# P·V of a cross-attention in four 32-column strips of the array instead of two of 64

## What is computed

```python
def _L0_xattn_ref(query, key, value, mask, Wq, bq, Wk, bk, Wv, bv, Wo, bo):
    Q = query @ Wq.T + bq
    K = key @ Wk.T + bk
    V = value @ Wv.T + bv
    Q, K, V = (z.reshape(b, -1, H, DK).transpose(0, 2, 1, 3) for z in (Q, K, V))   # H = 16, DK = 32
    scores = jnp.einsum('bhqd,bhkd->bhqk', Q, K) / jnp.sqrt(jnp.float32(DK))
    scores = jnp.where(mask == 0, -jnp.inf, scores)
    weights = jax.nn.softmax(scores, axis=-1)
    attn = jnp.einsum('bhqk,bhkd->bhqd', weights, V)          # "P·V"
    return attn.transpose(0, 2, 1, 3).reshape(b, -1, D) @ Wo.T + bo
```

## Time and profile before

| | before |
|---|---|
| median of 3 runs | 831.83 us (830.19 to 832.76) |
| the profiled execution | 832.76 us |
| its span | 831.0 us |
| TensorE busy | 787.1 us (95%), 8448 matmuls |
| VectorE busy | 624.2 us (75%) |
| ScalarE busy | 475.0 us (57%) |
| GpSimd busy | 274.7 us (33%) |

### The profile page before, as it was taken

How to read it: one execution, slowest core, us unless ns; L and a number is a source line. 1 busy time by engine, 2 the same in 40 slices (tenths; PEclk the granted TensorE clock), 3 DMA queues, 4 the chain that set the end, 5 groups by cost and what they waited for, 6 DMA issues and landing times.

```text
span 831.0 us, 21636 instructions
## 1 busy us (share of the span) xinstructions
PE 787.1 (95%) x8448; PEld 521.5 (63%) x8448; DVE 624.2 (75%) x971; ACT 475.0 (57%) x864; POOL 274.7 (33%) x411
## 2 busy tenths in 40 slices
PE   4999999999999999999999999994999999999994
PEld 2544455554445555545558544563999999999993
DVE  6866888889887767777765667988789688778850
ACT  3626666565765555566545034257578876876840
POOL 1422444433344333234421000031122474275342
PEclk9999999999999999999999999995999999999998
DMA  9444233444323344432323411113999898798201
GB/s 337 153 164 106 47 85 78 104 104 105 85 55 94 80 104 104 104 67 66 90 40 62 197 51 51 50 52 112 335 396 419 298 357 329 284 347 323 106 31 42
DMA packets 93148, 124.93 MB, mean 150 GB/s; under 512 B 75711, under 2 KB 78335, under 8 KB 81840
## 3 DMA queue, kind: packets, MB, share of 16 engines
q1 hardware_dynamic: 90528, 117.35, 44.1%
q0 software_dynamic: 2576, 7.02, 2.3%
HBM read 100.17 MB, written 6.88 MB: 129 GB/s over the span
## 4 chain that ended last, share of the span: by engine, by line
PE 74%; DVE 9%; ACT 5%; issue 4%; DMA 4%; POOL 2%; another core or an unknown queue 0%; POOLq 0%; ACTq 0%; DVEq 0%
PE bank L1333 56%; PE bank L1656 9%; PE bank L1445 3%; PE bank L1458 2%; DVE arena L837 2%; ACT arena L611 2%; DMA arena<-l_dram,arena 2%; DMA arena<-arena 2%; ACT arena L688 2%; DVE arena L976 2%; DVE arena L982 1%; PE bank L1346 1%; POOL arena L581 1%; POOL out L559 1%; ACT arena L797 1%
## 5 line engine op out<-in xcount | busy, mean ns | idle before, releaser
L1333 PE MATMUL bank<-arena 128*128 128x160 f16 (+8 forms) x4016 | 593.1, 308 | 7.8 <-DVE arena L1231 2.0
L1333 PEld LDWEIGHTS bank<-arena 128*128 128x128 f16 (+3 forms) x4016 | 339.2, 100 | 249.8 <-issue 13.2
L611 ACT ACTIVATE arena<-arena 128x2048 f16<-128x2048 f32 (+3 forms) x293 | 252.3, 905 | 11.7 <-DMA arena<-in_wq_t 6.7
L611 ACT ACTIVATE arena<-bank 128x512 f16<-128x512 f32 (+2 forms) x207 | 111.1, 543 | 206.5 <-PE bank L1333 131.8
L837 DVE SCALAR_TENSOR_TENSOR arena<-arena 128x2048 f16<-128x2048 f32 (+2 forms) x95 | 198.8, 2116 | 27.2 <-ACT arena L611 24.4
L837 DVE SCALAR_TENSOR_TENSOR arena<-bank,arena 128x512 f16<-128x512 f32 (+1 forms) x174 | 117.9, 685 | 70.6 <-ACT arena L611 66.9
L1656 PE MATMUL bank<-arena 128*128 128x160 f16 x1536 | 109.4, 233 | 1.0 <-issue 0.9
L1656 PEld LDWEIGHTS bank<-arena 128*128 128x128 f16 x1536 | 106.4, 98 | 1.8 <-issue 1.0
L559 POOL DMA_INDIRECT out<-arena x16 | 57.1, 3571 | 108.6 <-DVE arena L1263 106.2
L497 POOL TENSOR_TENSOR arena<-arena 32x1024 f16<-32x1024 f32 (+1 forms) x16 | 32.8, 2049 | 150.0 <-PE bank L1445 146.7
L688 ACT ACTIVATE arena<-arena 128x257 f32<-128x257 f32 x128 | 63.6, 498 | 25.6 <-DVE arena L984 25.6
(11 more groups left out here) (99 smaller groups left out, 418.1 us busy)
## 6 DMA issues: line engine op xcount, KB each, us to landing
arena<-in_w SPq DMA_DIRECT2D x64, 1024.0 KB, 5.7
arena<-in_ctx_t SPq DMA_DIRECT2D x16, 1024.0 KB, 5.2
arena<-in_awt SPq DMA_DIRECT2D x3, 1024.0 KB, 7.2
l_dram<-arena SPq DMA_DIRECT2D x4, 512.0 KB, 3.6
x_dram<-arena SPq DMA_DIRECT2D x1, 2048.0 KB, 12.4
arena<-in_x_t SPq DMA_DIRECT2D x2, 512.0 KB, 4.4
arena<-in_wq_t SPq DMA_DIRECT2D x1, 1024.0 KB, 6.6
arena<-in_x_t SPq DMA_DIRECT2D x1, 1024.0 KB, 8.7
```

Source lines behind the costliest of these rows:

```text
L611: return a.activation(dst, src, ACT.Copy, scale=scale)
L1333: last = m.matmul(out_ap, w, x, start=(n == 0), stop=(n == len(pairs) - 1))
```

## The change

P·V is cut into the 32-column strips of the array: each pair is four matmuls, each with 32 columns of w and the 32 columns of x of the same head, into the strip's 32 partitions of BG. `at` picks the head's place in x, since the scores lay their heads swapped in odd chunks. The bank then holds only wanted values, 256 columns. The evictions to `att_st` cover 128x256, and GpSimd moves each part with one copy of 128x256; two of its waits go, and `att_copied` counts one per step.

```diff
-        att_st = [xa.take([KC, PB, 2, S], F16) for _ in range(2)]
+        att_st = [xa.take([KC, PB, S], F16) for _ in range(2)]
...
-        pv_rows = BG[:].rearrange("p (c b h q) -> p c b h q", b=PB, c=KC, h=2)
+        pv_rows = BG[:, 0:PAIRS * S].rearrange("p (c b q) -> p c b q", b=PB, c=KC)
...
-            def attention_rows(m, last=False):
-
-                if last:
-                    pool.wait_ge(s["p_last_ready"], 2 * STEPS)
-                else:
-                    pool.wait_ge(s["vl_ready"], m + 2)
-                pool.sem_inc(s["pool_waits"], 1)
+            def attention_rows(m):
+
                 pool.wait_ge(s["pv_free"], m * 2 + 2)
                 pool.sem_inc(s["pool_waits"], 1)
                 for n in range(2):
-                    for r in range(HC):
-                        own = slice(r * DK, (r + 1) * DK)
-                        g.tensor_copy(attT[n][own, :, bass.ds(m * (PB * S), PB * S)]
-                                      .rearrange("p c (b q) -> p c b q", b=PB), att_st[n][own, :, :, r % 2, :]
-                                      ).then_inc(s["att_copied"], 1)
-                pool.wait_ge(s["att_copied"], m * (2 * HC) + 2 * HC)
-                pool.sem_inc(s["pool_waits"], 1)
+                    last = g.tensor_copy(attT[n][:, :, bass.ds(m * (PB * S), PB * S)],
+                                         att_st[n].rearrange("p c b q -> p c (b q)"))
+                last.then_inc(s["att_copied"], 1)
...
-                    act.wait_ge(s["att_copied"], from_zero(st * (2 * HC) - 2 * HC))
+                    act.wait_ge(s["att_copied"], from_zero(st - 1))
...
-                        cols = slice((c * PB + b) * HALF, (c * PB + b + 1) * HALF)
+                        cols = slice((c * PB + b) * S, (c * PB + b + 1) * S)
                         for n, (w, x) in enumerate(pairs):
-                            for r in range(2):
-                                own = slice(r * HALF, (r + 1) * HALF)
-                                at = (r + c) % 2
-                                last = m.matmul(BG[own, cols], w[:, own], x[:, at * HALF:(at + 1) * HALF],
+                            for r in range(HC):
+                                own = slice(r * DK, (r + 1) * DK)
+                                at = (r + 2 * (c % 2)) % HC
+                                last = m.matmul(BG[own, cols], w[:, own], x[:, at * S:(at + 1) * S],
                                                 start=(n == 0), stop=(n == len(pairs) - 1))
                     last.then_inc(s["pv_ps"], 1)
...
-            pe.wait_ge(s["att_copied"], STEPS * (2 * HC))
+            pe.wait_ge(s["att_copied"], STEPS)
```

More of the change, by code:

```diff
@@ L536, in _ @@
             step(STEPS - 1, nxt=False)
-            attention_rows(STEPS - 1, last=True)
+            attention_rows(STEPS - 1)
             def l2_lo(t):
```

## The result

| | before | after |
|---|---|---|
| median of 7 runs | 831.83 us (830.19 to 834.63) | 839.56 us (837.44 to 841.73) |
| ratio | | 1.0083, 95% interval 1.006 to 1.0104 |
| the profiled execution, its span | 832.76, 831.0 us | 838.28, 836.4 us |

The change makes the kernel 0.8% slower by the ratio, 7.7 us (0.9%) by the medians of seven and 5.4 us by the spans of the two profiled executions. Five further runs of the changed kernel on record lie between 836.55 and 841.33 us. The forecast was 828.9 us with a range from 826.5 to 836.

The account below looks back on a forecast made before the run. TensorE's work was taken to bound each step. Savings of 1.3 us (12 steps), 0.7 (steps 4, 6), 0.4 (step 15) and 0.5 (step 16), together 2.9, gave 828.9 us against the median of 831.83; range 826.5 to 836.

Parts of the forecast that it names:

- The bound: Whole step of the loop: it is as long as its TensorE work, 24.40 us; removing GpSimd's copies alone gives nothing.
- The strips overlap, 25 ns a group: P·V's matmuls: four strips run beside each other, a group takes 25 ns instead of 31.7, P·V 1.40 us.
- The supply of instructions: TensorE's queue in P·V: an instruction costs at most 5 ns, taken as 3; a group has eight instructions.
- My formula: P·V if supply binds: 448 instructions less 50 queued, times the time of each, plus 0.12; 2.1 us at 5 ns.
- What is late next: Scores after P·V wait for VectorE's fourth k_lo: start at 1.78 us, not 1.52, so 0.11 us saved a step, not 0.37.
- The chain of the evictions: Shorter evictions bring transposes for P·V's second half earlier; steps 4, 6 and 16 gain 0.6 us even without faster matmuls.
- 12 × 0.11: Steps 1 to 3, 5 and 7 to 14: each saves 0.11 us, together 1.3 us.
- supply becomes the bound: Rival, chance 0.18: TensorE's queue limits P·V from 4 ns an instruction; kernel 3 us slower at 5 ns, 10 at 6.
- My 3.7 us: Time the present P·V's 224 instructions would take by the skill page's 20-cycle floor, set against 1.89 us in the trace.

## Why the prediction was wrong, point by point

- **The bound was read rightly.** TensorE sets the step; removed copies and shorter evictions gave nothing in steps that had no stall.
- **The strips overlap, 25 ns a group: right.** Three strips run at 25.0 ns, and the first seven groups of the change do.
- **The supply of instructions: the step that failed in the steady state.** I bounded one instruction at 5 ns from the earlier trace rows and took 3; it is 4.17 (33.3/8). The bound held; choosing "nearer 3", from a register instruction elsewhere, did not. I had even named 4 ns as the point from which this decides, and stood 1 ns on the wrong side. My formula failed beside the rate: 398 × 4.17 ns + 0.12 is 1.78 us, exactly what I forecast, and 2.02 were measured. It let some 50 queued instructions pass in no time. In the trace the first 56 run at 25 ns a group, 0.18 us, the other 392 at 4.17 ns, 1.63 us, and the scores follow 0.2 us later: 2.0. Nor do the seven groups show a queue of 50: if 42 instructions came in while those 56 ran, 14 were in stock; the trace doesn't tell. That is 0.13 us a step lost where I had 0.11 gained, some 3 us of the distance.
- **What is late next: right to 0.01 us**, but only three strips show it, not the change.
- **The chain of the evictions: the time right, the worth open.** For steps 4, 6 and 16 I had 0.6 us without the matmuls. 0.72 are shown up to the last P·V; the 1.24 of its stall hang on a transpose that landed in 6.0 us instead of 4.4, which my sum didn't see: I took the 6.02 as given.
- **The first pass: missing altogether, and the largest term.** 5.3 us of the 6.6 by which the stage ends late come from a step that I counted as one of "12 × 0.11". I looked at middle steps and took all to be alike. The instruction packets of the profile's third part stood in front of me; I read instruction supply as the rate of a full queue and not as code that has to arrive. A row asked for here would have been: which block of code passes when, and how many instructions TensorE runs until then.
- **The rival "supply becomes the bound"** had the right sign and, for the steady part, the right mechanism. Its price of 3 us at 5 ns held only the rate, and by its formula 4.17 ns would have cost nothing; measured, the rate costs 14 × 0.13 = 1.8, and with the first pass the total passes the 836 at which the range ended.
- **The Trainium skill** page named above gives a floor of about 20 cycles an instruction, in that section without a clock. My 3.7 us took them at 1.2 GHz, 16.7 ns each; at 2.4 GHz they are 8.3 ns, which the 7.9 ns of the P·V of before hardly refute, but my bound of 5 ns from the earlier trace rows does, and so do the measured 4.17. I used the refutation of that floor as comfort. The same section describes the block fetch that cost 5.3 us, and says that this fetch is hidden because instructions are issued more slowly than they arrive. With the floor refuted, that reason was refuted too, and this should have led me to ask about the first pass.

## What to carry to other kernels

Splitting a matmul over more column strips pays until the instructions, loads included, reach 4.17 ns each; three strips of 32 columns ran at their own 25 ns, four are bound by the queue. Count instructions also where code runs for the first time: a stretch of some 450 short matmul instructions outran its own code and stood still for 3.5 us, and the low clock behind it took another 1.5, while the same stretch was harmless in all later passes. A first pass, a peeled step and the code behind a loop have to be costed by themselves. And an eviction that nobody waits for may stand ahead of work on which a transfer hangs: moving it behind gave 0.36% (0.23 to 0.5%) at no cost, of which the traces show 0.72 us in the loop to fit the shorter chain; the rest is open.

## What the runs showed of the hardware that I had not expected

- In P·V one TensorE instruction each 4.17 ns, matmul or weight load, with 32 as with 64 moving columns (2.02 and 2.03 us).
- A float32 matmul of 128x4 is issued as two passes; 64 of them delayed the first P·V by 22 us (101.87 for 79.94).
- Code comes in blocks: 256 instructions ahead left the stop in its place, 64 moved it by 64, and behind the loop a stop stood 256 behind the border that I had computed. TensorE went on 2.1 to 2.6 us after the packet of a missing block. Stops of 1.9 to 3.8 us in the first pass, 0.5 to 2.3 us behind the loop.
- The granted clock fell to 0.5 behind eight of the nine first-pass stops in the traces, also behind the one of 1.9 us, and cost some 1.5 us each (where the 24 matmuls of 128x512 lie wholly behind it, they took 6.86 to 7.04 us instead of 5.35). It didn't fall behind the first of the two when the first pass was written out (5.35), nor behind the stops of the last P·V, 1.15 us in the change and 2.3 with the first pass written out. Why these were spared stays open.
- Most DMA transposes of the same size landed 4.4 us after their issue, but one took 6.0 in the kernel before and one 6.1 in that of three strips. The traces don't tell why.
